# Turning normalised rows by DMA instead of by TensorE in the gate and routed stages of a two-layer kernel

## The reference

```
xf     = layernorm(x)                       # [8192, 256]
logits = xf @ gate_w.T                      # 8 experts
topk_logits, topk_idx = top_k(logits, 2)
comb   = softmax(topk_logits) put at topk_idx, zero elsewhere
for e in range(8):
    y   = silu(xf @ wg[e].T) * (xf @ wu[e].T) @ w_down[e].T     # 384 hidden
    out = out + comb[:, e:e + 1] * y
shared = silu(xf @ sg_gate.T) * (xf @ sg_up.T) @ sg_down.T      # 384 hidden
x = x + shared + out
```

## Time and profile before

| | |
|---|---|
| median of 3 runs | 3185.22 us (3173.67 to 3203.47) |
| the profiled execution's own time | 3194.49 us |
| its span, first to last instruction | 3192.8 us |
| busy share of the span: PE, DVE, ACT, POOL | 76%, 66%, 49%, 31% |
| mean granted TensorE clock | 0.845 |
| gate stage, steady part | 1186 to 1465 us of the span |
| routed stage, steady part | 1490 to 1945 us |

### The profile page before, as it was taken

How to read it: one execution, slowest core, us unless ns; L and a number is a source line. 1 busy time by engine, 2 the same in 40 slices (tenths; PEclk the granted TensorE clock), 3 DMA queues, 4 the chain that set the end, 5 groups by cost and what they waited for, 6 DMA issues and landing times. The chain is left out here.

```text
span 3192.8 us, 82493 instructions
## 1 busy us (share of the span) xinstructions
PE 2421.0 (76%) x26345; PEld 1424.0 (45%) x26345; DVE 2101.5 (66%) x5927; ACT 1572.3 (49%) x3621; POOL 988.0 (31%) x1303
## 2 busy tenths in 40 slices
PE   7917888888865657887999995881688888888336
PEld 4602222222214546776999994450233333333125
DVE  7827777777714556664545455991888888886278
ACT  5605666666650013332444443550477877778102
POOL 3503434433435016664666663340000000000005
PEclk9957878877876668998999997995798989999658
DMA  6521222222201113433443333653022212221123
GB/s 207 200 90 32 63 65 69 66 62 68 68 25 55 49 41 123 138 113 103 122 127 108 87 87 103 221 208 96 18 64 62 68 56 67 61 66 45 51 73 105
DMA packets 252029, 281.80 MB, mean 88 GB/s; under 512 B 98336, under 2 KB 184864, under 8 KB 251616
## 3 DMA queue, kind: packets, MB, share of 16 engines
q1 hardware_dynamic: 238656, 240.92, 24.8%
q0 software_dynamic: 12960, 35.54, 3.0%
HBM read 152.07 MB, written 123.62 MB: 86 GB/s over the span
## 5 line engine op out<-in xcount | busy, mean ns | idle before, releaser
L765 ACT ACTIVATE a_pr<-a_pst 128x384 f32<-128x384 f32 (+3 forms) x2176 | 935.6, 483 | 401.5 <-PE a_pst L789 362.8
L713 DVE TENSOR_REDUCE a_mx<-a_psc 128x1 f32<-128x384 f32 (+2 forms) x1152 | 592.2, 567 | 146.3 <-PE a_psc L789 137.2
L708 DVE CUSTOM_DVE_ANT_0 a_cut<-a_psc,row_mask 128x384 bf16<-128x384 f32 (+1 forms) x1024 | 499.7, 522 | 206.2 <-PE a_psc L789 170.3
L856 PE MATMUL a_po<-a_pr,a_ve 128*17 128x128 f32 (+3 forms) x10496 | 623.6, 329 | 1.6 <-ACT a_pr L765 1.0
L789 PE MATMUL a_psc<-a_ke,a_qe 52*128 52x128 f16 (+5 forms) x3072 | 410.8, 311 | 252.3 <-DMA a_ke<-mrow 113.9
L789 PE MATMUL a_pst<-a_qe,a_ke 53*128 53x128 f16 (+5 forms) x3072 | 398.8, 303 | 104.7 <-ACT a_pr L765 44.6
L687 POOL TENSOR_SCALAR_AFFINE_SELECT a_pr<-a_pr 128x512 f32<-128x512 f32 x448 | 275.0, 634 | 494.1 <-ACT a_pr L765 494.1
L1810 POOL TENSOR_TENSOR x_res<-x_res,t_bias 128x256 f32 (+1 forms) x64 | 44.5, 727 | 976.0 <-DVE t_xn L184 976.0
L789 PEld LDWEIGHTS a_pst<-a_qe,a_ke 53*128 53x128 f16 (+1 forms) x3072 | 122.6, 95 | 469.0 <-ACT a_pr L765 233.2
L789 PEld LDWEIGHTS a_psc<-a_ke,a_qe 52*128 52x128 f16 (+1 forms) x3072 | 130.7, 97 | 409.2 <-issue 162.1
L856 PEld LDWEIGHTS a_po<-a_pr,a_ve 128*17 128x17 f32 x10496 | 198.4, 98 | 238.6 <-issue 155.2
(11 more groups left out here) (221 smaller groups left out, 4538.3 us busy)
## 6 DMA issues: line engine op xcount, KB each, us to landing
a_qe<-qx SPq DMA_DIRECT2D x384, 64.0 KB, 2.6
a_ke<-kx SPq DMA_DIRECT2D x384, 64.0 KB, 2.6
e_xg<-xs SPq DMA_DIRECT2D x71, 258.0 KB, 3.0
vx<-p_vst SPq DMA_DIRECT2D x32, 544.0 KB, 3.1
a_ve<-vx SPq DMA_DIRECT2D x64, 272.0 KB, 3.1
ox<-a_ost SPq DMA_DIRECT2D x256, 68.0 KB
c_ot<-ox SPq DMA_DIRECT2D x32, 544.0 KB
qx<-p_stg SPq DMA_DIRECT2D x64, 256.0 KB, 3.3
```

The costliest lines, as they stand in the source:

```text
L708: dve.tensor_tensor_reduce(out=cut[:, n % 4, 0:width], in0=psc[n % RING][:, 0:width], in1=row_mask[:, at:at + width], scale=1.0, scalar=-3 ...
L713: dve.tensor_reduce(out.unsqueeze(1), psc[n % RING][:, 0:width], AXX, ALU.max)\
L765: act.activation(pr[s % SLOTS][:, h // 2, h % 2, 0:width], pst[k % RING][:, 0:width], ACT.Exp, scale=scale).then_inc(p_ready, 1)
L856: last = pe.matmul(po[h][32 * a:32 * a + VW, tok % CH:tok % CH + w], ve[g][:, t, a * VW:(a + 1) * VW], pr[s % SLOTS][:, a // 2, a % 2, col ...
```

## The change

Rows are split into 16-bit halves before they are turned, and a transposing DMA (`dma_start_transpose`) turns the halves.

In the gate stage ScalarE normalises (`row_hi`: four `Identity` activations with scale rstd and bias -mean*rstd, then one `Copy` of 128x1024 that makes the high half), VectorE makes the low half (`row_lo`, one instruction on 128x1024). Both halves lie side by side in `xrow`, which is what GpSimd now scatters, the same number of bytes a row. SyncE turns them with four DMAs a chunk (`turn`) of 128 rows x 512 values, from SBUF to SBUF, into `xt`, three chunks deep. `turn(s+2)` stands in SyncE's list ahead of the loads of turn s. ScalarE's `row_hi(s+2)` stands between the halves of turn s, ahead of its first `weight_hi`. VectorE's `row_lo(s+2)` stands in the middle of turn s, both its `weight_lo` now behind `hidden(s,1)`, and it takes over `low` for f = 2 from GpSimd. The transposes, `hi` and `lo` are gone.

In the routed stage SyncE turns each tile straight from DRAM with one DMA of 256 rows x 512 values into `xt`, three tiles deep, and loads the two extra columns with a second, small DMA (`col`). The transposes, `hi` and `lo` are gone here too.

```
@@ stage_route, sync
+            def turn(c):
+                r = c % XR
+                sp.wait_ge(row_low, ONE + c + 1)
+                if c >= XR:
+                    sp.wait_ge(gu_ready[FC - 1], ONE + 2 * (c - XR) + 2)
+                for t in range(TC):
+                    sp.dma_start_transpose(xt[:, r, :, t * P:(t + 1) * P], xrow[:, r, t, 0:2 * D]).then_inc(turned[r], 16)
+
             sp.dma_start(g32[:, :, :], gate_in).then_inc(g_loaded, 16)
-            for n in range(3):
+            for n in range(2):
                 load(n)
+            turn(0)
+            load(2)
+            turn(1)
             for s in range(NC + 2):
+                if s + 2 < NC:
+                    turn(s + 2)
                 for n in weight_parts(s):
                     load(n)
                 if s == NC:
                     sp.wait_ge(pads, ONE + 1)
+                    sp.wait_ge(cleared, ONE + 2)
@@ stage_route, gpsimd
-                            xn[:, c % XR, t, :], None).then_inc(scattered[c % XR], 16)
+                            xrow[:, c % XR, t, :], None).then_inc(scattered[c % XR], 16)
             def low(s, h):
-                for f in range(FC):
+                for f in range(FC - 1):
@@ stage_route, scalar
-            def hi(c):
-                for e in range(EC):
-                    act.wait_ge(turned, ONE + EC * c + e + 1)
-                    act.activation(xh[:, c % 2, e, :], pt[e][:, :], ACT.Copy, scale=XS).then_inc(hi_done, 1)
+            def row_hi(c):
+                if c:
+                    act.wait_ge(row_low, ONE + c)
+                for t in range(TC):
+                    ti = c * TC + t
+                    act.activation(xn[:, t, :], x_res[:, ti, :], ACT.Identity, bias=shift[:, ti:ti + 1],
+                                   scale=rstd[:, ti:ti + 1]).then_inc(normed, 1)
+                if c >= XR:
+                    act.wait_ge(scattered[c % XR], (c // XR) * TC * 2 * 16)
+                    act.wait_ge(turned[c % XR], ONE + (c // XR) * TC * 16)
+                act.wait_ge(normed, ONE + TC * (c + 1))
+                act.activation(xrow[:, c % XR, :, 0:D], xn[:, :, :], ACT.Copy, scale=XS).then_inc(row_high, 1)
...
                     high(s, h, 1)
                     high(s, h, 2)
+                    if h == 0 and s + 2 < NC:
+                        row_hi(s + 2)
                     for n in weight_parts(s)[h:h + 1]:
                         weight_hi(n)
@@ stage_route, vector
-            def norm(c):
...
-            def lo(c):
...
+            def row_lo(c):
+                dve.wait_ge(row_high, ONE + c + 1)
+                dve.scalar_tensor_tensor(out=xrow[:, c % XR, :, D:2 * D], in0=xn[:, :, :], scalar=XS,
+                                         in1=xrow[:, c % XR, :, 0:D], op0=ALU.mult, op1=ALU.subtract)\
+                   .then_inc(row_low, 1)
+            def low(s, h):
+                f = FC - 1
+                dve.wait_ge(hid_hi[f], ONE + 2 * s + h + 1)
+                dve.tensor_tensor(hl[:, h, f, :], hid[:, f, :], hh[:, h, f, :], ALU.subtract).then_inc(hid_lo[f], 1)
...
             for s in range(NC):
                 slots(s)
-                if s + 1 < NC:
-                    lo(s + 1)
                 hidden(s, 0)
                 if s > 0:
                     add_y(s - 1, 1)
-                for n in weight_parts(s)[0:1]:
-                    weight_lo(n)
+                low(s, 0)
+                if s + 2 < NC:
+                    row_lo(s + 2)
                 if s + 1 < NC:
                     top2(s + 1)
                 else:
                     table_of_tiles()
                 hidden(s, 1)
-                for n in weight_parts(s)[1:2]:
+                for n in weight_parts(s):
                     weight_lo(n)
+                low(s, 1)
                 add_y(s, 0)
-                if s + 2 < NC:
-                    norm(s + 2)
@@ stage_route, tensor: transpose(c) is gone
             def gates(c):
-                k = c % 2
-                pe.wait_ge(lo_done, ONE + EC * (c + 1))
+                r = c % XR
+                pe.wait_ge(turned[r], ONE + (c // XR + 1) * TC * 16)
@@ stage_routed, sync
                 row = sp.value_load(rt.row[0:1, j:j + 1], min_val=0, max_val=E * RS - SL)
+                if j >= GX:
+                    sp.wait_ge(gu_ready[FC - 1], ONE + j - GX + 1)
+                sp.dma_start_transpose(xt[:, j % GX, :, :], xs[bass.ds(row, SL), 0:2 * D]).then_inc(x_turned[j % GX], 16)
                 if j >= GR:
-                    sp.wait_ge(turned, ONE + j - GR + 1)
                     sp.wait_ge(addressed, ONE + AD * (j - GR + 1))
-                sp.dma_start(xg[:, j % GR, :, :], xs[bass.ds(row, SL), :].rearrange("(t p) w -> p t w", p=P))\
+                sp.dma_start(col[:, j % GR, :, :],
+                             xs[bass.ds(row, SL), 2 * D:2 * D + 4].bitcast(U32).rearrange("(t p) w -> p t w", p=P))\
                   .then_inc(loaded[j % GR], 16)
@@ stage_routed, tensor: transpose(j) is gone
             def up(j, expert, fs):
-                k = j % 2
+                g = j % GX
+                pe.wait_ge(x_turned[g], ONE + 16 * (j // GX + 1))
```

More of the change, by code:

```diff
@@ L43 @@
 XR = 3
+GX = 3
 RS = T + SL
@@ L1150, in stage_route @@
         made, cleared = sem("constants_made"), sem("before_cleared")
-        normed, turned, hi_done, lo_done = sem("normed"), sem("turned"), sem("hi_done"), sem("lo_done")
+        row_high, row_low = sem("row_high"), sem("row_low")
+        shifted, normed = sem("shifted"), sem("normed")
+        turned = [sem(f"turned{r}") for r in range(XR)]
         gated, ranked, routed = sem("gated"), sem("ranked"), sem("routed")
@@ L1370, in table_of_tiles @@
                 dve.wait_ge(counted, ONE + 1)
+                dve.memset(zeros, 0.0).then_inc(cleared, 1)
                 dve.tensor_copy(cnt[:, :], pg[:, 0, :]).then_inc(table, 1)
@@ L1426, in gate_weights @@
                 dve.wait_ge(table, ONE + 26)
+            dve.scalar_tensor_tensor(out=shift[:, :], in0=mean[:, :], scalar=-1.0, in1=rstd[:, :],
+                                     op0=ALU.mult, op1=ALU.mult).then_inc(shifted, 1)
             dve.memset(before[:, 0, :], 0.0).then_inc(cleared, 1)
-            dve.memset(zeros[:, :, :], 0.0).then_inc(cleared, 1)
+            row_lo(0)
             dve.wait_ge(g_hi, ONE + 1)
@@ L1432, in _ @@
                                      op0=ALU.mult, op1=ALU.subtract).then_inc(g_lo, 1)
-            norm(0)
+            row_lo(1)
             for n in range(3):
                 weight_lo(n)
-            lo(0)
-            norm(1)
             dve.wait_ge(made, ONE + 12)
-            dve.wait_ge(cleared, ONE + 2)
+            dve.wait_ge(cleared, ONE + 1)
             top2(0)
@@ L1467, in _ @@
         def _(pe):
-            def transpose(c):
-                pe.wait_ge(normed, ONE + TC * (c + 1))
-                pe.wait_ge(lo_done, ONE + EC * c)
-                for e in range(EC):
-                    for t in range(TC):
-                        last = pe.transpose(pt[e][:, t * P:(t + 1) * P], xn[:, c % XR, t, e * P:(e + 1) * P],
-                                            ident[:, :])
-                    last.then_inc(turned, 1)
             def gates(c):
-                k = c % 2
-                pe.wait_ge(lo_done, ONE + EC * (c + 1))
+                r = c % XR
+                pe.wait_ge(turned[r], ONE + (c // XR + 1) * TC * 16)
                 if c > 0:
@@ L1563, in stage_routed @@
         dest = sb("dest", [P, GR, 2], U32)
-        pt = [ctx.enter_context(nc.psum_tensor(f"{tag}_pt{k}", [P, EC, SL], F32)) for k in range(2)]
         pgu = [ctx.enter_context(nc.psum_tensor(f"{tag}_pgu{f}", [P, 2, SL], F32)) for f in range(FC)]
@@ L1567, in stage_routed @@
         loaded = [sem(f"loaded{g}") for g in range(GR)]
-        turned, hi_done, lo_done, addressed = sem("turned"), sem("hi_done"), sem("lo_done"), sem("addressed")
+        addressed = sem("addressed")
+        x_turned = [sem(f"x_turned{g}") for g in range(GX)]
         gu_ready = [sem(f"gu_ready{f}") for f in range(FC)]
@@ L1628, in _ @@
         def _(act):
-            def hi(j):
-                act.wait_ge(turned, ONE + j + 1)
-                act.activation(xh[:, j % 2, :, :], pt[j % 2][:, :, :], ACT.Copy, scale=XS).then_inc(hi_done, 1)
             def silu(j, f):
@@ L1699, in _ @@
         def _(pe):
-            def transpose(j):
-                g = j % GR
-                pe.wait_ge(loaded[g], ONE + 16 * (j // GR + 1))
-                if j >= 2:
-                    pe.wait_ge(lo_done, ONE + j - 1)
-                for e in range(EC):
-                    for t in range(2):
-                        last = pe.transpose(pt[j % 2][:, e, t * P:(t + 1) * P], xg[:, g, t, e * P:(e + 1) * P],
-                                            ident[:, :])
-                last.then_inc(turned, 1)
             def up(j, expert, fs):
-                k = j % 2
+                g = j % GX
```

(2 more changed lines are left out.)

77 lines of the change are left out of this document (26 added, 51 removed).

## The result

The changed kernel takes 3212.37 us (median of 16 runs, 3198.41 to 3225.78), the kernel before 3194.93 (16 runs, 3173.67 to 3207.47). The ratio is 1.0063 with an interval of 1.0046 to 1.0079: slower by 0.6%. The prediction had 3164 against a median of 3185.2, so a gain of 21 us; it is a loss of 17. On a second chip the same two kernels stand at 1.0002 (0.9979 to 1.0025), so of the sum only this can be said: between a gain of 0.2% and a loss of 0.8%, and not the forecast gain. (All ratios here are those of the record with their 95% intervals; they need not equal the quotient of the two medians.) What can be said of the two stages is much more, since both moved by far more than the sum.

The account below looks back on a forecast made before the run. TensorE was taken to bound the routed stage and to wait for VectorE's `norm` in the gate stage. Routed -30.5 and gate +9.5 gave -21 us, so 3164 against the median 3185.2; range 3130 to 3280.

Parts of the forecast that it names:

- two conditions: Routed stage: transposing DMA costs nothing if it lands within about 11.8 us and sustains one per 5.9 us.
- 0.3 us of room in front of `down`: Routed stage: without transposes, GpSimd's low half is ready at 1703.35, TensorE asks at 1703.7; the gain holds.
- The ring through SyncE's list: Gate stage: loads of turn s stand behind `turn(s+2)`, which waits for `row_lo(s+2)`; a closed cycle, 19.5 us a turn.
- tail turn without weights: Gate stage's last turns: ring open, 13.8 us against 16.18, twice, 5 us back.
- 16.5 + 4t: Gate stage: time of a turn, fixed part 16.5 us plus four transposing DMAs of t each; 19.5 us.
- What a turn costs: Gate stage: price t of one 128 KB transposing DMA, taken as 0.75 us between 0.37 and 1.36.
- what moves onto the path: Gate stage: sum of the new cycle's terms from the weights' landing, 16.0 us, 16.5 with handovers, before the four turns.
- t = 1.36: Gate stage: price of a transposing DMA in 256-byte pieces; turn 21.9 us, +43 instead of +14, 3193 us in all.
- Rival C: Gate stage: slow turning DMAs, 2.7 us each, turn 27.3 us, 3258 us; decides from 2.0 us on; chance 0.20.
- A: Gate stage: turning DMAs at the floor, fixed part up to 1.5 us shorter; 3128 to 3146 us; chance 0.22.
- B: Routed stage: room before `down` is gone, TensorE waits about as long as it transposed; 3185 us; chance 0.08.
- D: Both stages: 128x128 blocks follow one another on one DMA engine, 1.8 us each; about 4070 us; chance 0.06.

Follow-up runs that it names:

- experiment 8: Changed kernel with two instead of three buffers for the routed stage's turned rows: 3230.21 us, one run.
- Experiment 1: Changed kernel with the loads of turn s ahead of `turn(s+2)` in SyncE's list: 3133.21 us, ratio 0.9779 to the kernel before.
- experiment 7: Changed kernel with 70 empty matmuls on TensorE at the end of each of gate turns 0 to 11: 3259.61 us, ratio 1.0148 to the kernel before.
- experiment 6: On top of Experiment 1, first `weight_hi` ahead of `row_hi(s+2)` and first `weight_lo` ahead of `row_lo(s+2)`: 3137.08 us, ratio 0.9754 to the kernel before.
- experiment 3: Changed kernel with each gate-stage transposing DMA split into two of half the size: 3287.94 us, ratio 1.0258 to the kernel before.

## Why the prediction was wrong

Routed stage, right. 30.5 us were forecast, 29.2 came. The two conditions for costing the turning DMA at nothing held: it sustains one per 5.9 us, and experiment 8 shows that it lands in less. The 0.3 us of room in front of `down` was enough (a tile takes 5.89).

Gate stage, mechanism right. The ring through SyncE's list exists, ScalarE's largest idle time is the one before `weight_hi`, released by the weights' DMA, the queue waits for `row_lo`, TensorE falls to the lower clock once a turn, and a tail turn without weights takes 13.6 us (1486.72 to the next at 1500.35; forecast 13.8). Experiment 1 opens the ring and the whole loss is gone.

Gate stage, sizes wrong. The step that failed is the gate ring's sum, 16.5 + 4t = 19.5 us a turn, where 23.86 were measured, and both its terms failed. In "What a turn costs" t = 0.75 us came from an interpolation between a plain issue and a price of 256-byte pieces; it was not a price of bytes or of pieces at all but of instructions, 1.3 us each. And the fixed part, 16.5 us in "what moves onto the path", was 18.6. With t = 1.28 alone put right, the prediction's own sum gives a turn of 21.6 us and (21.6 - 18.33) x 12 - 35 = +4 us in all: no gain. The fixed part makes the rest. The terms, against one turn (from the weights' landing at 1282.99 to the next at 1307.52) and against the mean of the ten turns from 1236.05 on:

| term | forecast | one turn | mean of ten |
|---|---|---|---|
| `weight_hi` | 0.7 | 0.75 | 3.11 with the next row |
| half 1, up to the second `weight_hi` | 2.5 | 2.35 | |
| second `weight_hi` and its `weight_lo` | 1.85 | 1.85 | 1.85 |
| `low`, `add_y`, `slots` | 1.9 | 1.7 | 4.36 with the next row |
| `hidden(s+1,0)` to its last high half | 1.6 | 2.9 | |
| `row_hi` | 2.4 | 3.2 | 3.26 |
| `row_lo` | 1.5 | 1.45 | 1.25 |
| four turns in the queue | 3.0 | 5.2 | 5.4 |
| issue and landing of the load | 3.5 | 5.1 | 4.73 |
| handovers | 0.5 | in the terms | in the terms |
| sum | 19.5 | 24.5 | 24.0 |

The 4.5 us between 19.5 and 24.0 are 2.4 from the turns, 1.2 from issue and landing, 0.9 from the stretch up to the last high half, 0.9 from `row_hi`, less the 0.5 of handovers and 0.4 elsewhere. 11 x 4.4 = 48 us (with 23.86 for a turn) are nearly all of the 51 us by which the gate stage passed its forecast. The first of these four alone was inside the bounds (t = 1.36 stood as the upper one, with 3193 as its time); the other three, added without a range of their own, carried the result past that. Each copied a duration from a row of another state. The load's landing came from rows without turning DMAs in the queue. `hidden(s+1,0)` was costed from VectorE's and ScalarE's rows, but TensorE at the lower clock feeds them: in experiment 7, at the full clock, the stretch from the second `weight_lo` to `row_hi` took 3.62 us instead of 4.36, near the 3.5 of the forecast. And the four activations of `row_hi` were costed with a scale alone, where they have scale and bias.

Rival C priced the mechanism that came true ("slow turns"), with t = 2.7 and a point of decision at 2.0. The ring reached the turn of t = 1.8 by t = 1.3 and a longer fixed part. Its reason, writes in pieces of 2-byte elements, is not borne out: the price doesn't follow the bytes. A and B are out: the turns are not at the floor, and the routed stage kept its gain. D is out by the routed stage alone.

## What to carry to other kernels

A DMA that shares an issuing queue with others has two prices: the time it takes to land, which buffers hide, and the time for which it holds the queue, which nothing hides for what is behind it. Before moving a step to a DMA, look at what stands behind it in that queue and who waits for that; here two lines swapped were worth 8 us a turn, more than the change itself. An experiment that moves an instruction out of a ring must not move another into it (experiment 6), so add up the ring's parts in the trace before calling a theory dead. When a new cycle of waits is summed from rows, give every term a range, above all those whose engine will be in another state (another clock, a fuller queue) than in the row.

## What the runs showed of the hardware

- A transposing DMA of SyncE holds its queue for 1.25 us (128x256 values of 16 bits), 1.28 us (128x512) or 1.26 us (256x512 from DRAM), a plain one for 0.37 (258 KB): between 64 and 256 KB the number of instructions counts, not their size.
- With them the packets under 512 bytes went from 98336 to 226304 in the whole kernel, and the DMA share of the routed stage from 0.35 to 0.48. TensorE's waits there did not grow.
- Loads of 384 KB issued right behind four turning DMAs land after 4.7 us in the median, 3.5 without them; behind eight of half the size (experiment 3) it is 3.7. So it isn't the number of such DMAs that delays them; what does is not shown.
- ScalarE's `Identity` with a scale and a bias from a column takes 586 ns for 128x256 (float32 out), a `Copy` with a constant scale 413 (fp16 out).
- Keeping TensorE busy with empty matmuls brought each of `up` from 318 to 273 ns in the mean and a part of the ring from 9.3 to 8.6 us, but the turn stayed at 23.87 us, because `row_lo` (1.25 to 1.73 us) and the way from the turning DMAs to the weights' use (4.73 to 5.05 us) became longer by as much.
